# Moving the first gathers and combines of block 1 and 2 around the first root of attention 1

## What is computed

```python
x = x + _L0_xattn_ref(_layernorm(x), ctx_768, ...)
x = x + _L0_ffn_ref(_layernorm(x), ...)       # top 2 of 8 experts, and a shared one
x = x + _L1_xattn_ref(_layernorm(x), ctx_768, ctx_768, ...)
x = x + _L1_ffn_ref(_layernorm(x), ...)       # fp8-quantised product

def _L1_xattn_ref(query, key, value, ...):
    Qp = query @ Wq + bq
    K = _l2norm(key @ Wk + bk)
    V = value @ Wv + bv
    Q = _l2norm(Qp)                            # 16 heads of 16
    scores = jnp.einsum('bhqd,bhkd->bhqk', Q, K) * SCALE
    attn = jax.nn.softmax(scores, axis=-1)
    out = jnp.einsum('bhqk,bhkd->bhqd', attn, V) ... @ Wo + bo
    x = out + Qp
    return layernorm(x) * ln_gamma + ln_beta
```

## Time and profile before

| what | value |
|---|---|
| median of 3 runs | 986.73 us (984.72 to 989.7) |
| the profiled execution | 989.7 us, of which the traced span is 987.8 us |
| PE busy | 907.6 us, 92% |
| DVE busy | 765.5 us, 77% |
| ACT busy | 546.3 us, 55% |
| POOL busy | 361.2 us, 37% |
| experts end, attention 1 begins | 657.7 us |
| first score product of attention 1 | 681.5 us |

### The profile page before, as it was taken

One profiled execution on the slowest core, in us unless ns is written; L12 is line 12 of the kernel. 1 busy time (PEld: TensorE's weight loads), 2 busy tenths in 40 slices (PEclk: granted clock), 3 DMA queues, 4 the chain that ended last, 5 costly groups with the idle time before them and its releaser, 6 DMA issues. The chain is left out here.

```text
span 987.8 us, 17919 instructions
## 1 busy us (share of the span) xinstructions
PE 907.6 (92%) x5526; PEld 761.2 (77%) x5526; DVE 765.5 (77%) x1841; ACT 546.3 (55%) x1487; POOL 361.2 (37%) x414
## 2 busy tenths in 40 slices
PE   6899999999999999999899999988999999999535
PEld 5899999999999988888798899986655565554224
DVE  6698788788879877877567677866578988867988
ACT  4677557566656654444244444445555655654377
POOL 3134334333424336655402013237446455311330
PEclk9899999999999999999989999987999999999858
DMA  9999950000000023332234344441111011000003
GB/s 308 301 323 330 322 162 0 0 0 0 32 0 1 1 66 116 116 126 81 78 106 143 120 142 146 126 133 38 53 34 43 12 43 43 1 1 1 0 15 156
DMA packets 52761, 91.84 MB, mean 93 GB/s; under 512 B 5352, under 2 KB 27601, under 8 KB 52689
## 3 DMA queue, kind: packets, MB, share of 16 engines
q1 hardware_dynamic: 46544, 74.16, 23.8%
q0 software_dynamic: 6144, 16.79, 5.3%
HBM read 34.56 MB, written 56.36 MB: 92 GB/s over the span
## 5 line engine op out<-in xcount | busy, mean ns | idle before, releaser
L527 POOL TENSOR_TENSOR prob<-prob,row_inv 128x462 f32<-128x462 f32 (+1 forms) x96 | 83.8, 875 | 181.8 <-DVE row_inv L703 181.7
L890 PE MATMUL acc<-u,probT 128*128 128x256 f32 (+1 forms) x960 | 134.1, 289 | 1.0 <-DVE u L715 1.0
L587 ACT ACTIVATE prob<-score,neg_max 128x77 f32<-128x77 f32 x512 | 121.4, 352 | 15.0 <-DVE neg_max L697 14.7
L843 PE MATMUL score<-m,xnT 128*128 128x462 f32 (+1 forms) x576 | 124.5, 354 | 0.0
L890 PEld LDWEIGHTS acc<-u,probT 128*128 128x128 f32 (+1 forms) x960 | 119.4, 189 | 1.9 <-DVE u L715 1.4
L843 PEld LDWEIGHTS score<-m,xnT 128*128 128x128 f32 x576 | 97.9, 191 | 6.0
L1227 PE MATMUL py<-w1T,hidT 128*128 x426 | 93.9, 356 | 0.1
L577 ACT ACTIVATE probT<-tr 128x512 fp32r<-128x512 f32 (+1 forms) x96 | 52.1, 546 | 65.9 <-PE tr L829 65.5
L1575 POOL DMA_INDIRECT dispatched<-xn,slots x64 | 67.6, 1056 | 53.7 <-DVEq L1360 36.4
L2051 PE MATMUL score<-qT,kbd 128*128 128x512 f32 (+1 forms) x240 | 78.8, 438 | 0.2 <-ACT prob L2152 0.2
L1227 PEld LDWEIGHTS py<-w1T,hidT 128*128 128x128 f32 x426 | 72.6, 193 | 0.5 <-issue 0.5
(11 more groups left out here) (412 smaller groups left out, 2196.2 us busy)
## 6 DMA issues: line engine op xcount, KB each, us to landing
dispatched<-zeros SPq DMA_DIRECT2D x1, 33664.0 KB, 109.5
xn<-dispatched SPq DMA_DIRECT2D x71, 128.0 KB, 2.0
dispatched<-hid SPq DMA_DIRECT2D x71, 128.0 KB, 1.7
out<-x_res SPq DMA_DIRECT2D x7, 512.0 KB, 2.7
x_res<-in_x SPq DMA_DIRECT2D x1, 3072.0 KB, 15.4
consts<-in_L_ffn_W SPq DMA_DIRECT2D x8, 384.0 KB
consts<-in_L_ffn_Ws SPq DMA_DIRECT2D x3, 384.0 KB, 3.5
x_res<-in_x SPq DMA_DIRECT2D x2, 512.0 KB, 10.1
```

Of the source, the lines that this page charges most:

```text
L527: gp.tensor_tensor(pr, pr, row_inv[t % 2][:, heads(k)].unsqueeze(2).to_broadcast([P, BANK_HEADS[k], KEYS]), ALU.mult).then_inc(prob_ready, 1)
L587: last = act.activation(prob[t % 2][:, h * KEYS:(h + 1) * KEYS], score_of(t, k)[:, n * KEYS:(n + 1) * KEYS], ACT.Exp, bias=neg_max[t % 2][ ...
L843: last = pe.matmul(score_of(t, k)[:, 0:BANK_HEADS[k] * KEYS], xnT[blk][i][:, dc, j * P:(j + 1) * P], m[w][:, dc, cols(k)], start=(n == 0 a ...
L890: last = pe.matmul(acc[t % 2][:, 0:D], probT[t % 2][i][0:rows, c, :], u[k][0:rows, c, :], start=(c == 0 and q == 0), stop=(c == KCH - 1 an ...
```

## The change

The number of block 1's gathers issued during the experts goes from 2 to 3, and they wait for `y_out` of 66, 68 and 70 instead of 65 and 66. In attention 1, POOL has 5 instead of 6 gathers of block 1 left; the first three gathers of block 2 stand ahead of the root of block 0's queries instead of one behind it, and the other five stand behind both key spreads instead of three between them. DVE combines block 1's first half (k = 0) where it combined the second, and the second half directly ahead of the statistics; the columns of ones stand ahead of the two splits of the queries instead of behind them.

```diff
-LOADS_AT, WEIGHTS_AT, CONSTANTS_AT, NEXT_GATHER, NEXT_NORM, NEXT_SHIFT, NEXT_X, LATER_GATHER = 2, 8, 12, 34, 57, 64, 66, 65
-FIRST_PART = 2
+LOADS_AT, WEIGHTS_AT, CONSTANTS_AT, NEXT_GATHER, NEXT_NORM, NEXT_SHIFT, NEXT_X, LATER_GATHER = 2, 8, 12, 34, 57, 64, 66, 66
+FIRST_PART = 3
...
             for j in range(FIRST_PART):
-                gp.wait_ge(s["y_out"], LATER_GATHER + j)
+                gp.wait_ge(s["y_out"], LATER_GATHER + 2 * j)
...
                 gp.tensor_tensor(knorm[:, :], knorm[:, :], g["half"][0:KEYS, 0:B], ALU.pow).then_inc(s["norm_pow"], 1)
-                gp_root(gp, 0)
                 for k in range(YT_BUFS):
                     gp.wait_ge(g["stored"][k], 16 * len(range(k, TILES_B, YT_BUFS)))
-                gp_gather(gp, 2, 0, 1)
+                gp_gather(gp, 2, 0, 3)
+                gp_root(gp, 0)
                 gp_keys(gp, 0, 0)
                 gp_ln(gp, 1)
-                gp_gather(gp, 2, 1, TJ)
                 gp_keys(gp, 0, 1)
-                gp_gather(gp, 2, TJ)
+                gp_gather(gp, 2, 3)
...
-                dve_bias(dve, 0, 0)
-                dve_combine(dve, 1, 0)
-                dve_bias(dve, 0, 1)
+                for a in range(2):
+                    dve_bias(dve, 0, a)
                 dve_weights(dve, 2)
                 for a in range(2):
                     dve_queries(dve, 0, a)
                 dve_unit_keys(dve)
-                dve_combine(dve, 1, 1)
+                dve_combine(dve, 1, 0)
                 for f in range(DC):
                     dve_keys(dve, f)
                 for a in range(2):
                     dve_bias(dve, 1, a)
+                dve_combine(dve, 1, 1)
                 dve_stats(dve, 1)
-                for dc in range(DC):
-                    dve_split(dve, 0, 1, dc, qT[0])
+                dve_row_sums(dve)
+                dve_split(dve, 0, 1, 0, qT[0])
+                dve_split(dve, 0, 1, 1, qT[0])
                 dve_shift(dve, 1)
-                dve_row_sums(dve)
```

## The result

The changed kernel takes 994.25 us in the median, against 986.78 for the kernel before in the same comparison: a ratio of 1.0089, 95% interval 1.0068 to 1.0108, or 6.7 to 10.7 us. That is slower by more than the 0.5% that this kernel's measurement can tell, and well outside the range of the prediction. The profiled execution has a span of 995.0 us, 7.2 above the one of before.

A forecast was written before the change was run, and what follows sets the result against it. PE, 92% busy, was taken as the bound, with POOL's root setting the pace in attention 1's opening. Costs of 0 elsewhere and +0.75 there, +0.6 after the clock, gave 987.3 us from a median of 986.73; range 984.5 to 990.0.

The forecast's parts named there:

- the third gather in the experts: End of the experts: POOL's gather behind copy 70 reaches the barrier 0.06 us ahead of SP; cost 0, otherwise 0.1 to 0.6.
- The held gather: Opening of attention 1: the second of three gathers ahead of the root, held beside L2238, ends at 671.98, about 1.9 us.
- the long hold: Rival, opening of attention 1: the second gather is held through the combine as well, +2.3 us, 989.0; chance 0.16.
- The root at 1.04: Opening of attention 1: POOL's root starts at 673.31, the combine being over, and takes 1.04 us instead of 2.98.
- The upper bound of +2.3: Opening of attention 1: second gather held until 672.55, root to 675.85, ACT's scaling at 676.25, +2.3 us.
- the lower one: Opening of attention 1: second gather not held, third to 672.28, root to 673.35, ACT's scaling at 673.75, -0.2 us.
- The moved combine: Opening of attention 1: DVE's first combine moved back ends the keys' square sums about 0.95 us earlier, but gains nothing by itself.
- The waits for the stored tiles: Opening of attention 1: on POOL, these waits and the first issue of block 2's gathers cost 0.62 us behind the power.
- The DVE part: DVE between 674.6 and 680.5: statistics and splits end later, value products do not, no combine waits for rows; cost 0.
- the two cases that I gave: PE's clock, back at about 683.9: same moment wins back half the shift (+0.4), later by the same amount keeps +0.75; +0.6 taken.
- The one that ends slower: Rival, slower beyond 0.5%: long hold, longer 1.2 GHz level and late third gather, 2.3 + 1.5 + 0.6 = 4.4 us; chance 0.07.
- The rival that the gather isn't held at all: Rival, opening of attention 1: by the skill's rule the second gather runs unheld beside L2238, -0.2 us, 986.5; chance 0.16.

The follow-up runs named there:

- attention part alone: The changed kernel with the experts' gathers as before, two of them behind copies 65 and 66: 985.62 us, ratio 1.0002 to the kernel before.
- early drain: The changed kernel with one POOL drain added behind block 0's sum in the experts, where POOL waits for mean and variance: ratio 1.0053 to the kernel before.
- early drain with 66 to 68: The changed kernel with a POOL drain behind block 0's sum and its three gathers at copies 66, 67 and 68: 981.45 against 982.15 us, ratio 1.0002.

## Why the prediction was wrong

**The step that failed is the third gather in the experts**, "POOL arrives 0.06 ahead of SP: cost 0", with an upper bound of 0.6. The gather itself ran as forecast, 0.27 behind the 70th copy and 0.96 long, before SP's last store was out. What stands behind it on POOL was missing: "if POOL needs its own step to the barrier" was the right question, priced from nothing. The profile offered a bound: the row at 657.69 in the earlier trace rows gives 6.76 us between POOL's last gather and the start. I took all of it as waiting for SP. By the line fitted above, 6.22 of it were POOL's own drain and 0.15 the barrier; the cover was 657.69 less 657.31, about 0.4 us. The bound from both sides would have been 0 to 6.8, since nothing in the trace says that an engine was free during an idle time whose end is a barrier. 5.9 us, two thirds of the loss, come from there.

**The held gather was mis-sized.** I took 1.9 us by the row at 682.47, with the long hold as a rival at 0.16. It took 2.57 here and 3.55, 3.25 and 2.82 in the three other kernels with the same order (attention part alone, early drain, early drain with 66 to 68), each time until 0.83 or 0.84 behind the combine's end: held through the combine, as that rival said. The row at 682.47 had the same kind of instruction, but no combine directly behind its L2305; the better neighbour was the root's own 2.98, beside the same pair of DVE instructions.

**The root at 1.04 was wrong for a reason that no rival had.** Pushed back by the long gather, it started at 678.95, 0.22 behind the start of the second combine, and was held again, to 2.35. The upper bound of +2.3 had the root free. So had the lower one, which let it start at about 672.3, inside a combine that ends at 672.70. From the square sums to the query transposes the shift was +3.8 in place of +0.8.

**The moved combine gains something, against what I wrote.** The prediction let the square sums of the queries stay where they are, "behind the same PE products". They come 2.3 us earlier at the full clock, and 0.85 in the two profiled executions, both of which lost time to the lower clock. For the keys the room was smaller than said: the power comes 0.18 earlier (10.07 behind the start against 10.25) in place of 0.95, since at 1.2 GHz the second key bias waits for PE's products (2.09 at 670.84) and no longer for the combine. The waits for the stored tiles cost 0.19 and not 0.62.

**What held.** The DVE part cost nothing up to the scores: they come 5.68 behind the transposes, 5.80 before. No combine waited for its rows. From the start, though, DVE's value products come 1.6 later (24.42 against 22.79), because the splits ahead of them wait for the later transposes.

**The clock was half right.** It fell in the gap ahead of the transposes, as described, and of the two cases that I gave the worse came. PE's stretches answer to the earlier trace rows:

```profile
676.00:678.00 2.00, 0.07 (x1) 0.00 (x0) 2.00 (x6) 0.58 (x2) 1.70 (x2) 1.00 0.02 8
678.00:680.00 2.00, 0.00 (x0) 0.00 (x0) 2.00 (x6) 0.00 (x0) 1.98 (x2) 0.72 0.39 100
...
692.00:694.00 2.00, 2.00 (x8) 1.21 (x7) 0.00 (x0) 2.00 (x5) 1.39 (x3) 0.87 0.27 80
```

The level of 1.2 GHz ends at about 692.5, 30.0 behind the start against 26.2 before, so nothing of the shift was won back. What I had not counted at all is the lower clock right behind the barrier, which a late start brings with it.

**The rivals.** The one that ends slower named the right three places, a late third gather, a long hold and a longer level of 1.2 GHz, and gave each about the price of its bound: 4.4 in place of 8.3, with a chance of 0.07. Its lack was the drain. The rival that the gather isn't held at all failed in the four kernels with this order. By it stands what the Trainium skill, page "SBUF — State Buffer", section "Who interferes with whom", reports of one kind of such DVE instruction, that it didn't stall a DMA. The gather of 1.92 us beside L2305 alone, an instruction of that kind, speaks against it here; those of 2.57 and 3.55 us had a combine behind, and those of 0.99 and 1.00 met only the last 0.15 us of L2238.

**What the attention part costs** stays near the edge of what can be measured. From the start to the end the four traces with its order show 330.5 to 332.5 us, those with the order of before 328.3 to 330.5. Measured alone it is +0.2 us, with an interval of -3.1 to +3.4, and with the barrier's cost removed +0.2 again, -2.6 to +3.0. A cost of 0 to 2 us agrees with these. The changed kernel and the one with the early drain ask for 0.8 and 0.9 us at least over their starts, of which the lower clock behind a late start may be a part. No kernel here was faster than the one before.

## What to carry to other kernels

Before you put work late on an engine ahead of a barrier, ask what the barrier waits for on that engine besides the work: an idle time that ends at a barrier is no proof that the engine was free. On POOL the cost of its drain grows with the indirect DMAs issued since the last one, so put a drain of your own where POOL is idle anyway, and issue the last gather some 2 us before the others arrive, as the last of the drain experiments did. Where POOL work lies beside DVE work of two SBUF operands, take for the upper bound of a hold the end of the whole run of such instructions, and remember that what is pushed back may meet the next one.

## What the runs showed of the hardware

POOL's drain: 0.12 us with no indirect DMA issued, 0.80 after 8, 1.45 and 1.47 after 16, 2.83 after 32, 5.39 after 64 and 6.04 after 72, with nothing left under way in the cases of 64 and 72. The Trainium skill's page "VectorE: DVE Perf Modes", section "The DRAIN you can't avoid", puts the drains of a program's preamble and postamble at about 12 ns on every engine. No run here shows those; POOL's drains inside this program are far longer, so that figure doesn't carry over to them.

POOL's gathers and roots can be held beside DVE work of two SBUF operands; its small memsets weren't. Beside one such instruction, L2305, a gather of 0.96 us took 1.92; where a combine followed without a gap, 2.57 to 3.55, until some 0.83 us behind the combine's end.

The hold between DVE and POOL works both ways. POOL's key spread, begun 0.07 us ahead, stretched a combine from 1.66 to 4.12 us; begun 0.56 ahead, it stretched four small DVE copies (L2247) to 2.43 in the changed kernel.
